# Weighing seven pairs of attention steps per batch back to back, with four probability buffers instead of three

## The reference

```python
paths = jax.nn.sigmoid(x @ Wp + bp)                 # 8 heads x 5 levels
agree = pq * pk + (1.0 - pq) * (1.0 - pk)
sim = jnp.cumprod(agree, axis=-1).sum(axis=-1) / DEPTH
sim = jnp.where(mask[None, None], -jnp.inf, sim)    # causal
attn = jax.nn.softmax(sim, axis=-1)
V = (x @ Wv)
ctx = jnp.einsum('bhqk,bhkd->bhqd', attn, V)
x1 = _layernorm(x + ctx @ Wo)
h = jax.nn.silu(x1 @ wg.T) * (x1 @ wu.T)            # 768 hidden
out = _layernorm(x1 + h @ wd.T)
```

## Time and profile before

| what | value |
|---|---|
| median of 3 runs | 887.72 us (886.24 to 887.82) |
| the profiled execution | 885.52 us, its span 883.8 us |
| PE busy | 832.1 us, 94% of the span |
| DVE, ACT, POOL busy | 481.5, 454.1 and 233.2 us |
| share of PE in the chain that ended last | 87% |
| DMA | 71.09 MB, mean 80 GB/s |

### The profile page before, as it was taken

How to read it: one execution, slowest core, us unless ns; L and a number is a source line. 1 busy time by engine, 2 the same in 40 slices (tenths; PEclk the granted TensorE clock), 3 DMA queues, 4 the chain that set the end, 5 groups by cost and what they waited for, 6 DMA issues and landing times.

```text
span 883.8 us, 15437 instructions
## 1 busy us (share of the span) xinstructions
PE 832.1 (94%) x6146; PEld 412.3 (47%) x6146; DVE 481.5 (54%) x1021; ACT 454.1 (51%) x721; POOL 233.2 (26%) x266
## 2 busy tenths in 40 slices
PE   5299999999999999999999999999999999899986
PEld 3144355453644546454554536445364545344353
DVE  2934437645566545645376455665456553754466
ACT  2146654656456563656545564565636555364522
POOL 0011132223313232231322233132421313232224
PEclk9599999999999999999999999999999999999998
DMA  6750535005520336105360055303370062500001
GB/s 228 203 127 4 119 83 158 1 25 120 143 97 1 80 78 179 48 1 143 75 166 1 17 128 134 106 1 76 72 187 2 1 143 56 137 1 1 24 1 50
DMA packets 44362, 71.09 MB, mean 80 GB/s; under 512 B 3584, under 2 KB 21248, under 8 KB 44288
## 3 DMA queue, kind: packets, MB, share of 16 engines
q1 hardware_dynamic: 44288, 70.07, 30.1%
HBM read 53.28 MB, written 16.78 MB: 79 GB/s over the span
## 4 chain that ended last, share of the span: by engine, by line
PE 87%; DVE 6%; issue 2%; DMA 2%; ACT 1%; POOL 1%; SPq 1%; POOLq 0%; DVEq 0%; ACTq 0%
PE misc L821 17%; PE ctx_ps L786 16%; PE slot L764 15%; PE den_ps L786 13%; PE misc L833 9%; PE misc L740 7%; PE misc L798 6%; PE misc L749 2%; ACT probs L449 1%; DVE x1T_lo L600 1%; DMA query_stack<-phi_dram 1%; PE slot L821 1%; DVE ctx_raw L520 1%; PE misc L807 1%; DMA bp_sb<-in_bp_dram 1%
## 5 line engine op out<-in xcount | busy, mean ns | idle before, releaser
L449 ACT ACTIVATE probs<-slot 128x1024 f32<-128x1024 f32 (+3 forms) x384 | 290.1, 808 | 338.9 <-PE slot L764 338.6
L764 PE MATMUL slot<-query_stack,key_stack 128*128 128x512 f16 (+3 forms) x768 | 161.1, 331 | 16.3 <-DMA query_stack<-phi_dram 15.0
L786 PE MATMUL ctx_ps<-probs,vz_sb 128*32 128x512 f32 (+3 forms) x1536 | 164.5, 500 | 5.2 <-DVE ctx_raw L520 3.8
L402 POOL TENSOR_TENSOR work<-work 128x512 f16<-128x512 f32 x96 | 117.8, 1227 | 184.1 <-ACT work L467 184.1
L786 PE MATMUL den_ps<-probs,ones 128*32 128x512 f32 (+3 forms) x1536 | 159.6, 487 | 0.0
L388 POOL TENSOR_SCALAR_AFFINE_SELECT probs<-probs 128x512 f32<-128x512 f32 x128 | 82.0, 643 | 287.5 <-ACT probs L449 286.5
L821 PE MATMUL misc<-x1T_hi,w_parts 128*128 128x512 f16 x358 | 135.6, 379 | 6.3 <-DVE x1T_lo L600 6.0
L821 PE MATMUL misc<-x1T_lo,w_parts 128*128 128x512 f16 x358 | 135.7, 379 | 0.0
L610 DVE SCALAR_TENSOR_TENSOR work<-work,misc 128x512 f32<-128x512 f32 x89 | 61.1, 686 | 135.0 <-ACT work L461 135.0
L764 PEld LDWEIGHTS slot<-query_stack,key_stack 128*128 128x128 f16 x768 | 56.4, 98 | 167.5 <-issue 117.6
L833 PE MATMUL misc<-w_parts,work 128*128 128x256 bf16 x720 | 85.4, 276 | 3.9 <-POOL work L402 3.9
(11 more groups left out here) (74 smaller groups left out, 668.8 us busy)
## 6 DMA issues: line engine op xcount, KB each, us to landing
key_stack<-phi_dram SPq DMA_DIRECT2D x64, 256.0 KB, 5.7
query_stack<-phi_dram SPq DMA_DIRECT2D x64, 256.0 KB, 6.3
xT_sb<-in_xT_dram SPq DMA_DIRECT2D x8, 1024.0 KB, 5.0
x_sb<-in_x_dram SPq DMA_DIRECT2D x8, 1024.0 KB, 5.6
out_dram<-x SPq DMA_DIRECT2D x15, 512.0 KB, 3.5
phi_dram<-phi_hi SPq DMA_DIRECT2D x16, 256.0 KB, 2.1
phi_dram<-phi_lo SPq DMA_DIRECT2D x16, 256.0 KB, 2.4
work<-in_wgT_dram SPq DMA_DIRECT2D x1, 768.0 KB, 7.9
```

Source lines behind the costliest of these rows:

```text
L402: pool.tensor_tensor(hid_lo[:, n % M1, :], hid[:, n % HSLOTS, :], hid_hi[:, n % M1, :], ALU.subtract).then_inc(hid_lo_ready, 1)
L449: act.activation(probs[:, s % P_SLOTS, 2 * p:2 * p + 2, off:CH], slot[p][:, :, off:CH], ACT.Exp).then_inc(slot_drained[p], 1)
L764: mm = pe.matmul(slot[p][:, k, off:CH], key_stack[:, h, P * j:P * (j + 1)], query_stack[:, h, CH * c + off:CH * (c + 1)], start=True, stop ...
L786: mm = pe.matmul(sums[32 * k:32 * k + 32, off:CH], w, probs[:, s % P_SLOTS, k, off:CH], start=first, stop=final)
```

## The change

In seven steps of each batch (0, 2, 4, 11, 13, 15 and 22) the plan now holds no weighing. The step after each weighs two: the one that was left out and its own, behind its own filling. So the pairs weighed together are (22, 23 of the batch before), (0, 1), (2, 3), (9, 10), (11, 12), (13, 14) and (20, 21). Steps 0 of the first batch and 22 of the last one are exceptions, where nothing is paired; that leaves 54 pairs. `P_SLOTS` goes from 3 to 4. Nothing is added or removed otherwise.

```diff
-P_SLOTS = 3
+P_SLOTS = 4
...
         plan += between(b, i)
-        if LAG <= s < B * NS - 1:
-            b, i = divmod(s - LAG, NS)
-            plan += [("weigh", b, i)] + [("normalise", b, q) for q in range(NQ) if LAST[q] == i]
+
+        late = (0, 2, 4, 11, 13, 15, 22)
+        weighed = []
+        if i not in late or s >= B * NS - 2:
+            weighed = [s - LAG]
+            if i - 1 in late:
+                weighed = [s - LAG - 1, s - LAG]
+        for s2 in weighed if s < B * NS - 1 else []:
+            if s2 >= 0:
+                b, i = divmod(s2, NS)
+                plan += [("weigh", b, i)] + [("normalise", b, q) for q in range(NQ) if LAST[q] == i]
         return plan
```

## The result

| | before | after |
|---|---|---|
| median | 887.68 us (4 runs) | 895.65 us (894.25 to 897.08, 4 runs) |
| ratio | | 1.0089, 95% interval 1.007 to 1.0109 |
| profiled execution, span | 885.52, 883.8 us | 895.49, 893.8 us |
| PE busy | 832.1 us | 828.3 us |

The kernel became slower by 0.9%, while PE's busy time fell. The page of the kernel after: busy time of each engine, then the chain that ended last by engine.

What follows compares the result with a forecast made beforehand. PE's own work was taken to bound the kernel, busy 832.1 of 883.8 us. Middle batches +5.0, first +1.0 and last +1.7 gave +7.7 on 887.7: 895.4 us, range 885 to 900.

Steps and rivals of the forecast that it cites:

- The sum: Whole kernel: middle batches +5.0, first batch +1.0, last batch +1.7, together +7.7 us, giving 895.4 us, slower by 0.9%.
- the upper case: Whole kernel, with DVE's way to PE at 0.14 instead of 0.09 and ways in and out at 0.23: about 898.
- The saving: On PE, each pair saves one way into and one out of a weighing, 0.245 us; 13.0 us for 53 pairs.
- The three waits: PE on DVE, each middle batch: `turn_x1` at step 14 0.95 us, `turn_f` at step 23 0.88, `project` (steps 1 to 3) 0.73.
- The four harmless pairs: Middle batches: pairs (22, 23), (2, 3), (9, 10), (13, 14) cost no wait; a hidden one would be up to 0.5 us.
- The first batch: Five pairs save 1.2 us; steps 22 and 23 cost 0.88, step 14's scores waiting for exponentials 1.3: +1.0 in all.
- The last batch: Longer waits and slow clock through step 7 +2.25 us, step 14 +0.95, six pairs save 1.5: +1.7 in all.
- clock term: Last batch, behind PE's idle wait: half clock loses 1.4 us before and after; staying up after, the batch costs +0.3.
- The sign of being wrong: Whole kernel: the forecast is wrong if PE's waits on DVE grow by less than 13 us in all.
- only the ways in and out count: Rival, whole kernel: only savings entering and leaving weighings matter, 874.7 us; chance 0.12 for all below 886.
- `project` doesn't wait: Rival, steps 1 to 3: DVE finishes `ctxT` in time, total 888.7 to 890 us; chance 0.08 within 0.2%.
- each wait brings the clock down: Rival: new waits drop PE's clock once per batch, 1.4 us each, 905.2 us in all; chance 0.05.

## Why the prediction was right, point by point

**The sum.** +7.7 us were forecast, the medians differ by 8.0. That is closer than the terms deserve. By the traces, a middle batch took 1.03 to 1.04 more, not 0.84, and adding the traces' pieces (0.9 from step 6 of the first batch to step 7 of the next, 1.03 five times from step 7 to step 7, 2.6 to step 7 of the last batch, 0.3 to its last `normalise`) gives 9.0. The two profiled executions differ by 10.0; the rest is 0.7 ahead of step 6 of the first batch and 0.25 behind the last `normalise`. The medians' 8.0 carries the scatter of the runs, so they give the size of the effect only as 6 to 10 us (the interval of the ratio), and that they lie 0.3 from the forecast is partly luck. One smaller slip changes nothing: the upper case, given as about 898, adds up to 897.3 (0.05 at 21 waits and 0.8 less saved).

**The saving** was right: 0.245 forecast, 0.24 measured as (2.73 - 1.04) / 7, what the distance grew less than the waits explain, or (103.29 - 102.32) / 4 with four pairs.

**The three waits** were right in place, cause and order of size. Each was a little too small: 0.95, 0.88 and 0.73 forecast, 1.03, 0.94 and 0.76 measured. At the transposes the term that was mis-sized is the way from DVE to PE: I took 0.09 from a gate pair, but they start 0.15 after DVE's end, which makes 0.12 for the two places. At `project` that way was shorter than forecast, 0.06, and the start 0.71 late; the rest is that `project` itself took 0.05 longer. With the remaining 0.02 or so for rounding, that is 0.17 per batch of the 0.2 that the middle batches were short.

**The four harmless pairs** were right: no wait of PE appears at steps 1, 5, 12 or 16 of a middle batch, and with these four alone the distance is 102.32. The fourth buffer was right.

**The first batch** was right: the waits of the scores of step 14 on ACT there are new (0.64 and 0.31 in the list), and from the scores of step 13 to `turn_x1` PE takes 2.39, where 2.38 was worked out instead of 1.08: 1.3. In all it lost 0.9 by the traces, from its step 6 to step 7 of the next batch, where 1.0 was forecast; a wait of 0.36 ahead of its first gate pair went away too, which I hadn't counted.

**The last batch** was right in its list of waits: `project` waits 2.47 in the list (2.65 from the point at which it could have started, 2.75 forecast), the scores of step 3 0.53 and 0.20, those of step 5 0.74 and 0.42. By the traces the batch lost about 1.9 (2.6 to step 7 and 0.3 behind it, less 1.0 for steps 7 to 23 of the batch before), where 1.7 was forecast. Its clock term, that the clock falls before and after alike, held in this trace (0.53 behind the wait), but was luck, as the last section shows.

**The sign of being wrong.** "I am wrong if PE's waits on DVE grow by less than 13 us in all": in the list of waits they grow from 12.7 us (6.0 and 3.8 and 2.9) to 24.4, by 11.7. So by the list the sign says wrong, and the forecast of 0.8 to 0.9 for each `turn` was 0.64 and 0.56 there, the 0.7 of `project` 0.56. The waits had been worked out by starts, and the list counts brackets, which come out shorter, as shown above. By starts the bound is passed: 7 x (1.03 + 0.94) + 6 x 0.76 + 2.65, less the 2.4 by which `ctx_raw` fell, is 18.6. So the sign was set for the wrong quantity; the waits themselves are where they were forecast and a little longer.

**The rivals.** That only the ways in and out count would have needed waits under 1.72 per batch; they are 2.73. That `project` doesn't wait is refuted by its row. That each wait brings the clock down is refuted: the granted clock of the kernel after is 1.00 from 160 to 740 us, and the waits of five middle batches lie there.

## What to carry to other kernels

Regrouping work of one kind on the engine that bounds the kernel saved a small, fixed amount here, 0.24 us for each pair. But each regrouping also removes a cover somewhere: take the start at which the next step could run without it, and the end of what that step needs, both from the timeline before, and subtract; where the margin is shorter than the removed cover, the difference is paid each time. Pairs are not independent: one may give the cover that another one takes. Choosing four of seven by that subtraction turned +0.9% into -1.0%.

## What was unexpected of the hardware

The same idle stretch of PE can lower its clock or leave it. In the last batch of the kernel before PE idles 2.35 us before a weighing, and in the 3.5 us behind it the granted clock is 0.58. Here are the windows behind the wait at the same place in three other kernels: the full change (a wait of 2.47), then the one with only the pair (11, 12) (2.35), then the one with four pairs (1.49). After the window stand its length, the busy time of PE, PEld, DVE, ACT and POOL, then the granted clock, DMA share, GB/s.

```profile
762.50:766.00 3.50, 3.45 (x9) 2.80 (x10) 1.28 (x4) 0.00 (x0) 0.00 (x0) 0.53 0.67 182
```

```profile
760.20:763.00 2.80, 2.68 (x22) 1.09 (x23) 2.70 (x6) 0.48 (x2) 1.03 (x2) 1.00 1.08 215
```

```profile
745.70:749.00 3.30, 3.20 (x24) 1.56 (x25) 3.20 (x8) 0.66 (x2) 1.23 (x3) 1.00 1.08 222
```

In the earlier trace rows and in the first window here the clock is near the level of 1.2 GHz for most of 3.5 us; in the others it stays at 2.4 GHz, with the pair (11, 12) behind a wait of the same length by the same instruction as before. The kernel with only the pair (20, 21) also kept it (1.00 behind 2.35), the one with four buffers and nothing else did not (0.54 behind 2.35), and the one with DVE's part made shorter lost it behind 1.78 (0.55). (There waits of 0.53 and 0.20 stand just ahead, as they do in the full change.) A shorter wait lost the clock where a longer one kept it twice, so here the length of this wait alone doesn't decide, and a forecast can only give it a chance.

Between the same two points, from the restart to the start of `project`, PE takes 3.50 us in the kernel before and 2.30 with the pair (11, 12); in the full change `project` runs for 5.31 us instead of 3.72. So it costs 1.2 to 1.6 us when it happens.

Whether it is part of why whole runs scatter isn't shown, but the numbers point that way: of the 14 runs of the kernel before that stand beside the first experiments, eight have a mean granted clock of 0.978 and average 887.5 us, the other six have 0.980 to 0.982 and average 885.9.

In the middle batches, where PE's waits are up to 1.43 us in the list, it was not seen: from 160 to 740 us the granted clock is 1.00 with all seven pairs and with the pair (0, 1) alone.
